# Second cross attention of a two-block network: who issues the stores of the relative scores, and who multiplies one half in eight by the mask

## The chip, the cores and the metric

The kernel runs on one NeuronCore of a Trainium2 chip. The metric is the time of one execution on the device in microseconds. Three runs took 1361.1, 1364.61 and 1364.95 us; the median is 1364.61.

## The reference, cut to what matters

The network is one program: cross attention, linear attention, an attention with a mixture of experts, a second cross attention (relative positions, a mask), a multi-query attention and a second mixture. The change touches the fourth layer and, with one line, the second. What the fourth computes (x is 256 rows by 256, the context 4096 rows, 16 heads of 16 columns, float32):

```
q, k, v = x @ Wq + bq, y @ Wk + bk, y @ Wv + bv          # split into heads
content = einsum('bthd,bThd->bhtT', q + r_w_bias, k)
rel     = einsum('bthd,bThd->bhtT', q + r_r_bias, pe)    # pe from sinusoids @ Wp + bp
rel     = _relative_shift(rel)    # pad one column left, read the same memory with another row length
attn    = (content + rel) / sqrt(16)
attn    = attn * mask - 1e10 * (1 - mask)
out     = softmax(attn) @ v       # then @ Wo + bo
```

In the second layer (linear attention) the line moved is the addition of the norm's bias `beta` to x, which may be done at any time before the normed result is added.

## The kernel before, in words

The second cross attention is `cross1`. Its work is cut into 64 units: 16 heads, two blocks of 128 query rows, two halves of 2048 keys (`HALF`). `where(p, c)` gives for a unit its number n, its head and its place u = 0 to 3 in the head (U = 4). Each unit is handled in two parts of 1024 keys (`SUB`), part 0 and part 1.

All engines run the same list of slots (`slots`): slots -4 to 3 written out, then a hardware loop of six turns with eight slots each, then slots 52 to 67 written out. There is no planner: the order inside a slot is written by hand, per engine. In slot n:

- TensorE (`slot` at L1842): relative scores of unit n+3, part 1; content scores of unit n, part 0; for one unit in four the projection of new queries (L1800); the joining of the sums of unit n-4; transposes (`turn`, L1817) of unit n-3, part 0; relative scores of unit n+4, part 0; content scores of unit n, part 1; transposes of unit n-3, part 1; the product with the values (`weigh`, L1830) for both parts. The relative scores go to the PSUM tile `rel_ps`, the content scores to `cont_ps`, the transposes to `turn_ps`; there is one tile of each.
- ScalarE (L1911): copies the transposes of unit n-3, part 0 (L1909); the relative scores of unit n+4, part 0 (L1898); the transposes, part 1; the exponential of unit n-1 over both parts (L1903); the relative scores of unit n+4, part 1; for one unit in four turned weights (L1930).
- VectorE (L2013): sums of unit n-4 (L2005); adds content scores to the relative scores read back, unit n, part 0 (`add`, L1980); maximum of unit n-1, part 0, with the term of the mask added (`top_of`, L1991, a custom operation); keeps sums; add of unit n, part 1; maximum of unit n-1, part 1; joins both maxima and turns the sign (L1997), which releases the exponential; for one unit in four makes queries (L2052).
- GpSimd (L1943): multiplies both parts of unit n by the mask in SBUF (L1950), each when its add is done.
- SyncE: the relative shift is done through DRAM. `store` (L1713) writes a unit's relative scores with a row length of 4097, `read_back` (L1700) reads them with a row length of 4096 into `row`. In slot n SyncE reads back part 0 of unit n+2 (after the stores of its head that it overlaps have landed), then waits for ScalarE's copy and stores unit n+4, then reads back part 1 of unit n+2. Loads of keys and values stand between.

Before slot 0 VectorE copies the right halves of the relative scores itself (`evacuate_right`) and in slot -1 computes the second half of `minus`, the mask's additive term. At the end the last two units (`at_end`) have the transposes of part 1 in `rel_ps`, and VectorE copies them (L2042).

In `linear_attn` VectorE rotates the keys, adds a bias to the values, adds `beta` to x (L1061), waits for the query activation and rotates the queries.

## Time and profile before

| | |
|---|---|
| median of 3 runs | 1364.61 us (1361.1 to 1364.95) |
| profiled execution | 1368.14 us, span 1366.3 us |
| second cross attention, unit stage | about 707 to 1209 us of the span |
| busy in the span: TensorE, VectorE, ScalarE, GpSimd | 1127.7, 822.7, 893.6, 632.3 us |
| mean granted TensorE clock | 0.931 |

The table of an execution gives for each engine how long it was busy over the whole span of six layers with different limits. For a stage, the windows and the timeline are read instead: a row of a timeline has the start, the duration, the engine and the line, and, in brackets, how long the engine stood idle before and who released it. A duration on VectorE or GpSimd can contain time in which the operation was already issued and did not yet proceed.

### The profile page before, as it was taken

Reading aid. Unit: us, or ns where it says so; the run is one execution under the profiler, and the core shown is the slowest. Engines: PE = TensorE matmul, PEld = TensorE weight load, DVE = VectorE, ACT = ScalarE, POOL = GpSimd, SP = SyncE. Lnnn points to the kernel's source line nnn. Section 1 sums busy time; section 2 is a strip of 40 time slices with the busy share of each in tenths; the row PEclk is TensorE's granted clock in tenths of the full one; section 3 lists DMA queues with packets and bytes.
Section 4 is the critical chain, followed back from the end, with each engine's and each line's share of the span. In section 5 each row is a group of like instructions: output and inputs, shape, how many; then the busy total and the mean of one; then the engine's idle time right before and its main releaser. Section 6 shows DMA issues by size and latency. Waiting matters only on the chain. (4 is left out here: it accounts for less than half of the span.)

```text
span 1366.3 us, 25496 instructions
## 1 busy us (share of the span) xinstructions
PE 1127.7 (83%) x8423; PEld 690.0 (50%) x8423; DVE 822.7 (60%) x1502; ACT 893.6 (65%) x1204; POOL 632.3 (46%) x297
## 2 busy tenths in 40 slices
PE   7677877859999859989977888888888888857798
PEld 3344443433444346678852444544455444434687
DVE  5688888870111166462235787888878888835312
ACT  3599999978999624433323788888888888524110
POOL 2277887850000005000004899999999999800000
PEclk9899999979999878989985899999999999878899
DMA  7875555538654070024458999999899999433140
GB/s 244 246 231 130 132 122 130 131 98 165 119 99 89 13 254 8 1 78 153 154 218 283 309 308 323 325 333 325 311 319 334 328 322 317 152 114 127 47 139 8
DMA packets 97052, 257.53 MB, mean 188 GB/s; under 512 B 11193, under 2 KB 41306, under 8 KB 85467
## 3 DMA queue, kind: packets, MB, share of 16 engines
q1 hardware_dynamic: 96992, 256.79, 60.3%
q8 instruction: 32, 0.52, 0.2%
q14 instruction: 28, 0.22, 0.1%
HBM read 165.31 MB, written 91.92 MB: 188 GB/s over the span
## 5 line engine op out<-in xcount | busy, mean ns | idle before, releaser
L1950 POOL TENSOR_TENSOR xb_row<-xb_row,w_mask 128x1024 f32<-128x1024 f32 x128 | 419.2, 3287 | 240.0 <-DVE xb_row L1980 238.7
L1980 DVE TENSOR_TENSOR xb_row<-xb_cont_ps,xb_row 128x1024 f32<-128x1024 f32 x128 | 156.7, 1224 | 83.2 <-PE xb_cont_ps L1773 73.3
L1773 PE MATMUL xb_rel_ps<-xb_kk,xb_qq 32*128 32x512 f32 x496 | 148.9, 678 | 35.0 <-ACT xb_out L1898 33.3
L561 DVE TENSOR_REDUCE xa_stats<-xa_b_ps 128x1 f32<-128x1024 f32 x128 | 155.8, 1219 | 27.2 <-PE xa_b_ps L477 25.8
L1991 DVE CUSTOM_DVE_ANT_0 xb_row<-xb_row,xb_minus 128x1024 f32<-128x1024 f32 x128 | 170.9, 1335 | 0.0
L1903 ACT ACTIVATE xb_row<-xb_row,xb_ntop 128x2048 f32<-128x2048 f32 x64 | 128.3, 2005 | 51.1 <-DVE xb_ntop L1997 51.1
L1773 PE MATMUL xb_cont_ps<-xb_kk,xb_qq 32*128 32x512 f32 x528 | 160.2, 684 | 1.5 <-DVE xb_qq L2052 1.1
L880 ACT ACTIVATE xa_probs<-xa_psT,xa_t_now 128x1024 f32<-128x1024 f32 x128 | 141.2, 1114 | 18.4 <-PE xa_psT L837 18.3
L1898 ACT COPY xb_out<-xb_rel_ps 128x1024 f32<-128x1024 f32 x124 | 124.7, 1005 | 39.8 <-PE xb_rel_ps L1773 26.8
L1909 ACT COPY xb_turned<-xb_turn_ps 128x1024 f32<-128x1024 f32 x126 | 127.5, 1012 | 26.9 <-PE xb_turn_ps L1817 24.8
L529 ACT ACTIVATE xa_exps<-xa_b_ps,xa_stats 128x1024 f32<-128x1024 f32 x128 | 140.7, 1102 | 6.6 <-DVE xa_stats L561 6.6
L1817 PEld LDWEIGHTS xb_turn_ps<-_ident,xb_row 128*128 128x128 f32 x1008 | 116.4, 149 | 56.0 <-issue 56.0
L1817 PE MATMUL xb_turn_ps<-_ident,xb_row 128*128 128x128 f32 x1008 | 139.3, 283 | 5.5 <-ACT xb_turned L1909 4.6
L647 POOL TENSOR_TENSOR xa_rest<-xa_exps 128x1024 f32<-128x1024 f32 x48 | 90.9, 1894 | 92.0 <-ACT xa_exps L529 86.7
L1830 PE MATMUL xb_sum_ps<-xb_turned,xb_vhead 128*17 128x128 f32 x2048 | 82.2, 279 | 37.1 <-ACT xb_turned L1909 36.0
L1420 POOL TENSOR_TENSOR b_tc<-b_raw,w_waves 128x512 f32<-128x512 f32 x4 | 5.1, 1274 | 216.1 <-ACT b_raw L1406 216.1
L477 PE MATMUL xa_b_ps<-xa_k,xa_q 96*128 96x512 bf16 x256 | 70.6, 388 | 24.3 <-ACT xa_exps L529 13.9
L539 ACT ACTIVATE xa_squares<-xa_exps 128x1024 f32<-128x1024 f32 x80 | 84.4, 1055 | 3.0
L810 PE MATMUL xa_sums<-xa_probs,xa_vhead 128*17 128x256 f32 x1024 | 81.1, 390 | 0.2 <-ACT xa_probs L880 0.2
L498 PE MATMUL xa_b_ps<-xa_wv,xa_ctxT 128*128 x512 | 67.3, 286 | 15.1 <-ACT xa_exps L529 15.1
L1830 PEld LDWEIGHTS xb_sum_ps<-xb_turned,xb_vhead 128*17 128x17 f32 x2048 | 45.5, 97 | 67.0 <-ACT xb_turned L1909 54.4
L498 PEld LDWEIGHTS xa_b_ps<-xa_wv,xa_ctxT 128*128 128x128 f32 x512 | 61.3, 196 | 31.0 <-ACT xa_exps L529 26.4
(367 smaller groups left out, 1823.9 us busy)
## 6 DMA issues: line engine op xcount, KB each, us to landing
xb_row<-rel_scores SPq DMA_DIRECT2D x128, 512.0 KB, 6.3
rel_scores<-xb_out SPq DMA_DIRECT2D x32, 1024.5 KB, 5.6
rel_scores<-xb_out SPq DMA_DIRECT2D x32, 1024.0 KB, 5.6
b_e_w<-in_L_ffn_e_w SPq DMA_DIRECT2D x32, 513.0 KB, 3.4
w_w<-in_L_ffn_w SPq DMA_DIRECT2D x24, 512.0 KB, 4.9
xa_k<-first_parts SPq DMA_DIRECT2D x24, 384.0 KB, 5.1
value_rows<-xa_values SPq DMA_DIRECT2D x16, 544.0 KB, 6.1
xb_kk<-key_blocks SPq DMA_DIRECT2D x17, 512.0 KB, 7.8
```

Of the source, the lines that this page charges most:

```text
L498: mm = nc.tensor.matmul(out[:, n * P:(n + 1) * P], ctxT[:, k, at:at + P], wv[:, bass.ds(it, 1), k, :], start=(k == 0), stop=(k == KC - 1))
L529: nc.scalar.activation(exps[:, u % 4], ps[:, slot % 4], ACT.Exp, scale=-1.0, bias=stats[:, c % 2, 0, u:u + 1], accum_out=stats[:, c % 2, 1 ...
L561: nc.vector.tensor_reduce(stats[:, c % 2, 0, u:u + 1], ps[:, slot % 4], AX, ALU.min).then_inc(s["min_ready"], 1)
L880: nc.scalar.activation(probs[:, g % 4].rearrange("p c n -> p (c n)"), ps[:, g % 2], ACT.Exp, scale=t_now[:, b:b + 1]).then_inc(probs_ready, 1)
L1773: mm = nc.tensor.matmul(out[:, k * BANK:(k + 1) * BANK], qq[rows, b, kind, t * P:(t + 1) * P], kk[rows, b, half], start=True, stop=True)
L1817: mm = nc.tensor.transpose(out_ps[:, k * P:(k + 1) * P], row[:, held(c), at:at + P], f.ident[:])
L1830: mm = nc.tensor.matmul(sum_ps[at:at + DV, 0:P], vhead[:, b, half * NCH // 2 + part * CPS + k, :], turned[:, part, k, :], start=(part == 0 ...
L1903: nc.scalar.activation(row[:, held(c)], row[:, held(c)], ACT.Exp, bias=ntop[:, u:u + 1]).then_inc(s["exp_done"], 1)
L1909: nc.scalar.copy(turned[:, part].rearrange("p k n -> p (k n)"), turn_ps[:]).then_inc(turned_sb[part], 1)
L1950: nc.gpsimd.tensor_tensor(row[:, held(c), at:at + SUB], row[:, held(c), at:at + SUB], mask[:, t, half * HALF + at:half * HALF + at + SUB], ...
L1980: nc.vector.tensor_tensor(row[:, held(c), at:at + SUB], cont_ps[:], row[:, held(c), at:at + SUB], ALU.add).then_inc(s["cont_out"], 1)
L1991: nc.vector.tensor_tensor_reduce(out=row[:, held(c), at:at + SUB], in0=row[:, held(c), at:at + SUB], in1=minus[:, t, half * HALF + at:half ...
```

## The change

- SyncE no longer stores the relative scores. ScalarE issues the store of unit n+4 in slot n, after its second copy of that unit's relative scores, and first waits for that copy (and, for the first four units, for VectorE's). SyncE's slot holds both read-backs one behind the other, and the loads as before.
- For the last unit of each head (u = 3), part 1, VectorE adds the content scores in PSUM (`cont_ps`), waits for itself, and multiplies the sum by the mask into `row`; GpSimd leaves that part out. That is one of eight halves of a head.
- The last slots: from slot 64 on, TensorE transposes both parts of a unit first in the slot. The last three units instead of two have part 1 in `rel_ps`; of these ScalarE copies the first, VectorE the last two.
- The second half of `minus` is computed in slot -4 instead of slot -1.
- In the linear attention the addition of `beta` stands ahead of the wait for the key activation.

```
--- before.py
+++ after.py
@@ -1052,13 +1052,13 @@
             step(nc.vector.tensor_scalar(red[:], red[:], PI_BELOW, -PI_BELOW, ALU.min, ALU.max))
...
             dve.wait_ge(s["loaded"], 80)
+            step(nc.vector.tensor_tensor(f.x[:], f.x[:], gain[:, 1].unsqueeze(1).to_broadcast([P, NT, D]), ALU.add))
             dve.wait_ge(s["k_gelu"], 1)
...
             dve.sem_inc(s["v_sb"], 1)
-            step(nc.vector.tensor_tensor(f.x[:], f.x[:], gain[:, 1].unsqueeze(1).to_broadcast([P, NT, D]), ALU.add))
             dve.wait_ge(s["q_gelu"], 1)
...
             dve.sem_inc(s["qrot_ready"], 1)
@@ -1625,7 +1625,7 @@
             names = ("small_loaded", "var_ready", "root_ready", "dve_steps", "xn_ready", "xnT_mm", "xnT_sb",
...
                      "rel_mm", "rel_out", "cont_mm", "cont_out", "masked", "halves_max", "top_ready",
-                     "exp_done", "turned", "weighed", "sums_sb", "gathered", "sums_read", "zero_set", "top_begun", "top_kept", "row_free")
+                     "exp_done", "turned", "weighed", "sums_sb", "gathered", "sums_read", "zero_set", "top_begun", "top_kept", "row_free", "added_here")
             s = {n: f.sem("b_" + n) for n in names}
...
             turned_sb = [f.sem(f"b_turned_sb{n}") for n in range(2)]
@@ -1683,7 +1683,15 @@
 
...
 
+                return isinstance(n, int) and n >= UNITS - 3
+
+            def by_vector(n):
+
                 return isinstance(n, int) and n >= UNITS - 2
+
+            def masked_here(u, part):
+
+                return u == U - 1 and part == 1
 
...
 
@@ -1710,19 +1718,6 @@
                     sp.dma_start(row[:, held(c):held(c) + 1, columns], src.rearrange("h p n -> p h n")
...
 
-                def store(p, c):
-                    n, head, u, b, t, half = where(p, c)
-                    sp.wait_ge(s["rel_out"], 2 * n + 3)
-                    if isinstance(n, int) and n < U:
-                        sp.wait_ge(s["fill_out"], n + 1)
-                    rows = rel_rows[bass.ds(head, 1), t * P:(t + 1) * P, :]
-                    if half == 0:
-                        dst, src = rows[:, :, 0:HALF + 1], out0
-                    else:
-                        dst, src = rows[:, :, HALF + 1:PITCH], out1
-                    sp.dma_start(dst.rearrange("h p n -> p (h n)"), src[:]).then_inc(rel_stored[u], 16)
-
-                rel_rows = rel_dram[:, 0:S * PITCH].rearrange("h (r n) -> h r n", n=PITCH)
                 shifted = rel_dram[:, S:S + S * S2].rearrange("h (r n) -> h r n", n=S2)
...
 
@@ -1738,15 +1733,9 @@
                         if n is None or n > U:
...
                         load_values(p, c + U)
-                    begins = n is not None and n == -2
                     if runs(n, 2):
-                        read_back(p, c + 2, 0, first=n is not None and n + 2 < ROWS_HELD)
-                    if runs(n, 2) and begins:
-                        read_back(p, c + 2, 1, first=True)
-                    if runs(n, U):
-                        store(p, c + U)
-                    if runs(n, 2) and not begins:
-                        read_back(p, c + 2, 1, first=n is not None and n + 2 < ROWS_HELD)
+                        for part in range(2):
+                            read_back(p, c + 2, part, first=n is not None and n + 2 < ROWS_HELD)
 
...
                     b = c // U % 2
@@ -1840,6 +1829,7 @@
                                      ).then_inc(s["gathered"], 1)
...
                 def slot(p, c, n):
+                    ending = isinstance(n, int) and n >= UNITS
                     if runs(n, U - 1) and (n is None or n > 0):
...
                     if c % U == 0 and (n is None or n < UNITS):
@@ -1849,6 +1839,9 @@
                         pe.wait_ge(k_loaded[(c // U + 1) % 2], 16 * (p + (c // U + 1) // 2 + 1))
...
                         content(p, c, 0)
+                    if ending and runs(n, -BEHIND):
+                        turn(p, c - BEHIND, 0)
+                        turn(p, c - BEHIND, 1)
                     if runs(n, -BEHIND - 1):
...
                     if n is None or n >= 0:
@@ -1856,7 +1849,7 @@
                             make_queries(2 * p + c // U + 2, c // U % 2)
...
                         bring_together(p, c - BEHIND - 1)
-                    if runs(n, -BEHIND):
+                    if runs(n, -BEHIND) and not ending:
                         turn(p, c - BEHIND, 0)
...
                         relative(p, c + U, 0)
@@ -1867,7 +1860,8 @@
                     if runs(n, 0):
...
                     if runs(n, -BEHIND):
-                        turn(p, c - BEHIND, 1)
+                        if not ending:
+                            turn(p, c - BEHIND, 1)
                         weigh(p, c - BEHIND, 0)
...
 
@@ -1897,6 +1891,20 @@
                     first = isinstance(n, int) and n < U
...
 
+                rel_rows = rel_dram[:, 0:S * PITCH].rearrange("h (r n) -> h r n", n=PITCH)
+
+                def store(p, c):
+                    n, head, u, b, t, half = where(p, c)
+                    act.wait_ge(s["rel_out"], 2 * n + 3)
+                    if isinstance(n, int) and n < U:
+                        act.wait_ge(s["fill_out"], n + 1)
+                    rows = rel_rows[bass.ds(head, 1), t * P:(t + 1) * P, :]
+                    if half == 0:
+                        dst, src = rows[:, :, 0:HALF + 1], out0
+                    else:
+                        dst, src = rows[:, :, HALF + 1:PITCH], out1
+                    nc.scalar.dma_start(dst.rearrange("h p n -> p (h n)"), src[:]).then_inc(rel_stored[u], 16)
+
                 def exponentials(p, c):
...
                     act.wait_ge(s["top_ready"], n + 1)
@@ -1906,19 +1914,22 @@
                     n, head, u, b, t, half = where(p, c)
...
                     act.wait_ge(s["weighed"], 2 * n + part + 1)
-                    nc.scalar.copy(turned[:, part].rearrange("p k n -> p (k n)"), turn_ps[:]).then_inc(turned_sb[part], 1)
+                    src = rel_ps if at_end(n) and part == 1 else turn_ps
+                    nc.scalar.copy(turned[:, part].rearrange("p k n -> p (k n)"), src[:]).then_inc(turned_sb[part], 1)
 
...
                         evacuate(p, c + U, 0)
-                    if runs(n, -BEHIND) and not at_end(where(p, c - BEHIND)[0]):
+                    if runs(n, -BEHIND) and not by_vector(where(p, c - BEHIND)[0]):
                         copy_turned(p, c - BEHIND, 1)
...
                         evacuate(p, c + U, 1)
+                    if runs(n, U):
+                        store(p, c + U)
                     if turns_weights(n, c):
...
 
@@ -1945,11 +1956,14 @@
                         return
...
                     for part in range(2):
+                        if masked_here(u, part):
+                            continue
                         at = part * SUB
+                        halves_done = 2 if masked_here(u, part + 1) else 1
                         pool.wait_ge(s["cont_out"], 2 * n + part + 2)
...
                                                 mask[:, t, half * HALF + at:half * HALF + at + SUB],
-                                                ALU.mult).then_inc(s["masked"], 1)
+                                                ALU.mult).then_inc(s["masked"], halves_done)
 
...
 
@@ -1977,6 +1991,14 @@
                     dve.wait_ge(rel_back[u][part], 16 * (head + 1))
...
                     at = part * SUB
+                    if masked_here(u, part):
+                        nc.vector.tensor_tensor(cont_ps[:], cont_ps[:], row[:, held(c), at:at + SUB], ALU.add
+                                                ).then_inc(s["added_here"], 1)
+                        dve.wait_ge(s["added_here"], head + 1)
+                        nc.vector.tensor_tensor(row[:, held(c), at:at + SUB], cont_ps[:],
+                                                mask[:, t, half * HALF + at:half * HALF + at + SUB],
+                                                ALU.mult).then_inc(s["cont_out"], 1)
+                        return
                     nc.vector.tensor_tensor(row[:, held(c), at:at + SUB], cont_ps[:], row[:, held(c), at:at + SUB],
...
 
@@ -1984,6 +2006,8 @@
 
...
                     dve.wait_ge(s["masked"], 2 * n + part + 1)
+                    if masked_here(u, part):
+                        dve.wait_ge(s["cont_out"], 2 * n + part + 2)
                     if part == 0 and isinstance(n, int) and n == 0:
...
                     dve.sem_inc(s["top_begun"], 1)
@@ -2013,10 +2037,10 @@
                 def slot(p, c, n):
...
                         evacuate_right(c + U)
+                        if n == -U:
+                            set_minus(1)
                         if makes_queries(n, c):
                             make_queries(1, 1)
-                        if n == -1:
-                            set_minus(1)
                     if runs(n, -BEHIND - 1):
...
                     if runs(n, 0):
@@ -2032,7 +2056,7 @@
                     if n is None or n >= 0:
...
                             make_queries(2 * p + c // U + 2, c // U % 2)
-                    if runs(n, -BEHIND) and at_end(where(p, c - BEHIND)[0]):
+                    if runs(n, -BEHIND) and by_vector(where(p, c - BEHIND)[0]):
                         copy_last_turned(p, c - BEHIND)
```

## Rows read from the trace of the kernel before

**Rows 1.** Windows, one turn of the loop: stretch, length, busy us by engine, clock, DMA share, GB/s
```profile
922.40:979.30 56.90, 47.94 (x536) 28.14 (x536) 47.10 (x85) 47.57 (x43) 52.66 (x17) 1.00 0.94 325
```

**Rows 2.** Timeline, one slot: start us, us, engine line op out<-in, idle before it
```profile
930.00 0.19 PEld L1773 LDWEIGHTS xb_rel_ps<-xb_kk,xb_qq 32*128 32x128 f32 x2 [1.27 <-ACT xb_out L1898]
...
931.24 1.23 DVE L1980 TENSOR_TENSOR xb_row<-xb_cont_ps,xb_row 128x1024 f32<-128x1024 f32 x1 [0.97 <-PE xb_cont_ps L1773]
...
932.38 1.22 DVE L1991 CUSTOM_DVE_ANT_0 xb_row<-xb_row,xb_minus 128x1024 f32<-128x1024 f32 x1
...
933.64 0.21 DVE L1997 TENSOR_SCALAR xb_ntop<-xb_top 128x1 f32<-128x1 f32 x1
...
933.89 2.01 ACT L1903 ACTIVATE xb_row<-xb_row,xb_ntop 128x2048 f32<-128x2048 f32 x1 [0.67 <-DVE xb_ntop L1997]
...
935.80 0.99 ACT L1898 COPY xb_out<-xb_rel_ps 128x1024 f32<-128x1024 f32 x1
...
936.84 0.19 PEld L1773 LDWEIGHTS xb_rel_ps<-xb_kk,xb_qq 32*128 32x128 f32 x2 [0.48 <-ACT xb_out L1898]
```

**Rows 3.** The same timeline, from the next slot to the fourth exponential
```profile
937.00 1.01 ACT L1909 COPY xb_turned<-xb_turn_ps 128x1024 f32<-128x1024 f32 x1
...
938.15 1.06 PE L1817 MATMUL xb_turn_ps<-_ident,xb_row 128*128 128x128 f32 x8
...
939.25 1.81 DVE L1991 CUSTOM_DVE_ANT_0 xb_row<-xb_row,xb_minus 128x1024 f32<-128x1024 f32 x1
939.33 1.01 ACT L1909 COPY xb_turned<-xb_turn_ps 128x1024 f32<-128x1024 f32 x1 [0.21 <-PE xb_turn_ps L1817]
...
940.97 0.70 PE L1773 MATMUL xb_cont_ps<-xb_kk,xb_qq 32*128 32x512 f32 x2
...
941.35 2.00 ACT L1903 ACTIVATE xb_row<-xb_row,xb_ntop 128x2048 f32<-128x2048 f32 x1 [1.01 <-DVE xb_ntop L1997]
...
942.02 0.73 PEld L1800 LDWEIGHTS xb_both<-xb_xnT,xb_wturn 128*128 128x128 f32 x4 [0.76 <-issue]
...
943.13 1.07 PE L1817 MATMUL xb_turn_ps<-_ident,xb_row 128*128 128x128 f32 x8
...
944.31 0.70 PE L1773 MATMUL xb_rel_ps<-xb_kk,xb_qq 32*128 32x512 f32 x2
...
948.22 2.00 ACT L1903 ACTIVATE xb_row<-xb_row,xb_ntop 128x2048 f32<-128x2048 f32 x1 [0.55 <-DVE xb_ntop L1997]
...
955.49 2.01 ACT L1903 ACTIVATE xb_row<-xb_row,xb_ntop 128x2048 f32<-128x2048 f32 x1 [0.94 <-DVE xb_ntop L1997]
```

**Rows 4.** Timeline of GpSimd where the stage starts
```profile
737.89 2.34 POOL L1950 TENSOR_TENSOR xb_row<-xb_row,w_mask 128x1024 f32<-128x1024 f32 x1 [1.12 <-DVE xb_row L1980]
741.36 3.25 POOL L1950 TENSOR_TENSOR xb_row<-xb_row,w_mask 128x1024 f32<-128x1024 f32 x1 [1.13 <-DVE xb_row L1980]
```

**Rows 5.** Page, part 5: GpSimd's mask products, out<-in xcount, busy, mean ns
```profile
L1950 POOL TENSOR_TENSOR xb_row<-xb_row,w_mask 128x1024 f32<-128x1024 f32 x128 | 419.2, 3287 | 240.0 <-DVE xb_row L1980 238.7
```

**Rows 6.** Timeline of SyncE's queue: a store, a load of keys
```profile
951.29 0.35 SPq L1723 DMA_DIRECT2D rel_scores<-xb_out  x1
...
966.71 1.15 SPq L97 DMA_DIRECT2D xb_kk<-key_blocks  x1
```

**Rows 7.** Timeline of the last slots
```profile
1167.10 1.23 DVE L1980 TENSOR_TENSOR xb_row<-xb_cont_ps,xb_row 128x1024 f32<-128x1024 f32 x1 [1.74 <-DMA xb_row<-rel_scores]
...
1189.15 2.15 DVE L1991 CUSTOM_DVE_ANT_0 xb_row<-xb_row,xb_minus 128x1024 f32<-128x1024 f32 x1
...
1197.49 2.00 ACT L1903 ACTIVATE xb_row<-xb_row,xb_ntop 128x2048 f32<-128x2048 f32 x1
...
1208.43 0.17 DVE L2010 TENSOR_SCALAR xb_o_all<-xb_both 128x17 f32<-128x17 f32 x1 [0.49 <-PE xb_both L1839]
```

**Rows 8.** Timeline of linear attention
```profile
484.94 0.43 DVE L1024 SCALAR_TENSOR_TENSOR la_kr<-la_k,la_rope 128x256 f32<-128x256 f32 x1 [1.54 <-ACT la_k L1012]
...
488.66 0.69 DVE L1061 TENSOR_TENSOR _x<-_x,la_gain 128x512 f32<-128x512 f32 x1
```

More of the change, by code:

```diff
@@ L1054, in _ @@
             dve.wait_ge(s["loaded"], 80)
+            step(nc.vector.tensor_tensor(f.x[:], f.x[:], gain[:, 1].unsqueeze(1).to_broadcast([P, NT, D]), ALU.add))
             dve.wait_ge(s["k_gelu"], 1)
@@ L1060, in _ @@
             dve.sem_inc(s["v_sb"], 1)
-            step(nc.vector.tensor_tensor(f.x[:], f.x[:], gain[:, 1].unsqueeze(1).to_broadcast([P, NT, D]), ALU.add))
             dve.wait_ge(s["q_gelu"], 1)
@@ L1740, in slot @@
                         load_values(p, c + U)
[L1741 removed]
                     if runs(n, 2):
[L1743 to L1749 removed]
+                        for part in range(2):
+                            read_back(p, c + 2, part, first=n is not None and n + 2 < ROWS_HELD)
                 def load_values(p, c):
@@ L1851, in slot @@
                         content(p, c, 0)
+                    if ending and runs(n, -BEHIND):
+                        turn(p, c - BEHIND, 0)
+                        turn(p, c - BEHIND, 1)
                     if runs(n, -BEHIND - 1):
@@ L1858, in slot @@
                         bring_together(p, c - BEHIND - 1)
-                    if runs(n, -BEHIND):
+                    if runs(n, -BEHIND) and not ending:
                         turn(p, c - BEHIND, 0)
@@ L1908, in copy_turned @@
                     act.wait_ge(s["weighed"], 2 * n + part + 1)
-                    nc.scalar.copy(turned[:, part].rearrange("p k n -> p (k n)"), turn_ps[:]).then_inc(turned_sb[part], 1)
+                    src = rel_ps if at_end(n) and part == 1 else turn_ps
+                    nc.scalar.copy(turned[:, part].rearrange("p k n -> p (k n)"), src[:]).then_inc(turned_sb[part], 1)
                 def slot(p, c, n):
@@ L1915, in slot @@
                         evacuate(p, c + U, 0)
-                    if runs(n, -BEHIND) and not at_end(where(p, c - BEHIND)[0]):
+                    if runs(n, -BEHIND) and not by_vector(where(p, c - BEHIND)[0]):
                         copy_turned(p, c - BEHIND, 1)
@@ L1921, in slot @@
                         evacuate(p, c + U, 1)
+                    if runs(n, U):
+                        store(p, c + U)
                     if turns_weights(n, c):
```

63 lines of the change are left out of this document (37 added, 26 removed).

## The prediction, made before the changed kernel was run

> **What bounds the kernel now.** I read the page's totals first. No engine is busy for the whole span, so the share of busy time decides nothing, and the stretch that the change touches has to be read by itself: the second cross attention, 707 to 1209 us, and in it the even part from 765 to 1165 us. The table by windows shows one turn of its loop of eight units (the other five from 808 to 1150 us are alike): 56.9 us, 28.45 us for one round of four units (one head), TensorE's clock at its upper level (granted 1.00), VectorE 47 us busy, ScalarE 47.5, TensorE 48, GpSimd 52.7, DMA 94% [rows 1]. At first sight GpSimd and the DMA engines are the wall. The timelines of single engines show something else.
>
> *The loop of waits.* I followed one slot back from what ended its waits [rows 2]. TensorE's relative and content scores of one half start at 930.00; VectorE adds the content scores at 931.24, takes the maximum at 932.38, joins the halves at 933.64; ScalarE's exponential starts at 933.89, its copy of the relative scores at 935.80, and TensorE's next pair of scores, which needs the PSUM tile that this copy empties, at 936.84, "waiting for ACT xb_out". Each step starts when the one before ends. It is a closed loop, once per slot, and one turn is 936.84 - 930.00 = 6.84 us. Nothing in it is GpSimd's or a DMA. Four turns are 27.36 of the 28.45 us of a round.
>
> *What is on top of it.* The other start of the exponential in these rows is 7.46 later (933.89 to 941.35), then 6.87 (948.22) and 7.27 (955.49) [rows 3]. In the long slots the maximum takes 1.81 instead of 1.22 [rows 2, 3]. Its partner is GpSimd's product with the mask: 2.34 us while VectorE takes no maxima, 3.25 once it does [rows 4]. So the maximum (two SBUF inputs) and the mask product take turns: one slot costs the pair 2 x 1.22 + 2 x 2.34 = 7.12 us, which is 56.9/8 = 7.11. The add of a PSUM and an SBUF operand beside the same GpSimd work stays at 1.22 [rows 2, 3]. The Trainium skill says so too ("SBUF — State Buffer", section "Who interferes with whom" and the one on the two sides of SBUF): VectorE and GpSimd share one pair of ports as an exclusive lock, a VectorE operation with two SBUF inputs takes it, the loser is blocked whole. By that rule alone the change is worth its lock time; it makes the rival A below, and the trace agrees with the lock (0.91 us more on each mask product) but not with the conclusion: the loop of 6.84 is there with the lock free.
>
> *A second chain.* Between the slots of units 0 and 1 of a head TensorE is tight as well [rows 3]: scores at 936.84, ScalarE's copy of turned weights 937.00 (ends 938.01), transposes 938.15, copy 939.33, scores 940.97, query projection 942.02, transposes 943.13 to 944.20, next pair of scores 944.31. That is 7.47 us with no gap over 0.25.
>
> **The change part by part.**
>
> *The product on VectorE (16 units, the second half of the last unit of each head).* Removed: 16 of GpSimd's 128 mask products, 3.29 us each by their mean [rows 5]. GpSimd is on the path only through the lock. Added, between the add and the maximum of the unit before, on the very loop of 6.84: one more VectorE operation from PSUM and SBUF to SBUF, and a wait for the add. The like of it is the add, 1.22 us; adjacent VectorE operations start 1.14 apart (931.24 to 932.38 [rows 2]), and a wait for one's own predecessor gives up that overlap and some hundredths: I take 1.30, bounds 1.14 and 1.40. Behind it on VectorE stand the maximum and the joined maximum, and ScalarE's exponential waits for them. ScalarE idles 0.67 us before that exponential, but it idles *for* this chain, so that idle time hides nothing. VectorE's own idle time of 0.97 us lies before the add, while it waits for TensorE, and can't be used either. So the slot of the fourth unit goes from 6.84 to 8.14.
>
> *What the lock gives back.* In the slot of unit 3 the maximum waited for nothing (1.22), so there is nothing to give. The slot after it (unit 0) loses its wait for the lock, 1.81 - 1.22 = 0.59, because GpSimd has no second product to do and the add comes early. But the second chain holds that slot at 7.47, so the gain is 0. In the slot of unit 2 the add is late because two query operations stand ahead of it; its maximum keeps its wait (the slot is 7.27, 955.49 - 948.22). Bounds: 0 to 0.43 a round, if that wait goes too; I take 0.
>
> *ScalarE issues the stores.* SyncE's issue of this very store takes 0.35 us [rows 6]. On ScalarE it stands after the second copy of relative scores, waits for that copy to be finished, and then the copy of turned weights follows. The trace shows no DMA issued by ScalarE; I take 0.35 and 0.10 for the wait, 0.45. Bounds: 0.05 (only the wait, an issue that the engine's data path doesn't see) and 1.25 (SyncE's issue of keys is 1.15 [rows 6], and 0.10). It isn't on the loop of 6.84: the pair of scores starts meanwhile. In most slots it eats ScalarE's idle time. In the slot of unit 0 it is on the second chain, ahead of the copy at 937.00, less some 0.05 of gap before the transposes: 7.47 + 0.40 = 7.87. SyncE loses 64 issues and its waits for the copies; the read-backs go out sooner. VectorE waits for a read-back hardly ever (the adds wait for TensorE), and the DMA engines carry the same bytes, so the even part gains nothing by it. The Trainium skill ("DMA: Bandwidth & Descriptors", on issuing engines not being separate queues) says that issuing from a second engine saves only the sequencer's time. No row here has a second queue, and the sum doesn't use it.
>
> *Sum of a round:* unit 0 7.87, unit 1 6.87, unit 2 7.27 (both as they are), unit 3 8.14, together 30.15 against 7.47 + 6.87 + 7.27 + 6.84 = 28.45. That is +1.70. The even part, 765 to 1165, is 400/28.45 = 14 rounds: +23.8 us. The bounds: product 1.14, store nothing, lock wait of unit 2 gone: +0.71, 14 times is +10. Product 1.40, store 1.25: the second chain takes 1.15 and the slots of units 1 and 2 lose their slack of about 0.3 each: 1.40 + 1.15 + 0.6 = +3.1, 14 times is +44; I hold that the copy's issue is near the store's own row and keep about +35 as the upper end.
>
> *Start.* The slot of the first head's unit 3 gets its product outside of the 14 rounds: +1.3. The second computation of "minus" moves from slot -1 to slot -4. It is one operation of about the length of VectorE's wait there for TensorE, and the first add followed TensorE's scores, not it: 0.
>
> *Last slots.* The exponential of unit 62 starts at 1191.59 behind a maximum that took 2.15 [rows 7]: the product ahead of it adds 1.3 and takes most of that wait, so it starts at about 1192.3. Then on ScalarE its 2.0 and two copies of 1.0 (the second no longer waits for the first, since unit 61 now uses both PSUM tiles): the last exponential starts at 1196.3 instead of 1197.49. Weighing of unit 61 ends at 1197.0, two transposes of 1.07 at 1199.2, VectorE's copy and the weighing at 1201.2, transposes of unit 63 at 1203.4, copy 1.22, weighing, sums and joining another 2.1: the last operation ends at 1206.7 instead of 1208.6 [rows 7]. That is -1.9, bounds 0 and -3. The add at 1167.10 waits 1.74 us for a read-back [rows 7]; SyncE issues it sooner now, as it no longer waits for copies: -1.7, bounds 0 and -1.8.
>
> *Linear attention.* The bias added to x (0.69 us) moves from between two steps of the path, into a wait of 1.54 us for the key activation [rows 8]: -0.7, bounds 0 and -0.7.
>
> Total: +23.8 + 1.3 - 1.9 - 1.7 - 0.7 = +20.8 us. The profiled execution took 1368.1 us (span 1366.3 and 1.8 around it) and would take 1389. It is 3.5 us above the median of the runs shown, 1364.6. I take the difference over to the median: 1385.4 us, +1.5%.
>
> **The rivals.**
>
> A. *The lock and GpSimd were the wall.* If each slot's length is the lock's time, a round loses 2 mask products of 2.34 out of eight units, so 2.34 in a round: 26.1; the DMA engines at 94% set a floor of 0.94 x 28.45 = 26.7. Gain 1.7 a round, 24 in all, and 3 at the ends: 1338 us. If it goes only as far as the loop of 6.84 (27.36 a round, the product hidden), the gain is 15 + 3: 1346. For it: 7.12 against 7.11, GpSimd 92% busy. Against it: a slot with an undisturbed maximum has no idle step in the loop, and the product is laid on it. It is right from the point where VectorE can do the product before its content scores would be late anyway.
>
> B. *Nothing measurable.* With the low bounds (+10) and the ends giving more than I count (-6 with their bounds, +1.3 for the first head less), or the second chain closing up because its copy finds ScalarE free earlier: about +2, 1367 us.
>
> C. *The store on ScalarE is dear.* An issue of about 1.2 us instead of 0.35, since the two queues' issues get in each other's way or the address work lands on ScalarE: +35, less 3 at the ends: 1397 us. For it: SyncE's issues reach 1.15 [rows 6]. Against it: the store's own issues there are all near 0.35.
>
> D. *The product does not reach the loop because the transfers set the pace after all* (94% share): then every slot stays at 7.11 and only the ends change: 1361 us. Against it: the waits of the adds are for TensorE.
>
> **How the numbers follow.** Forecast case 0.64, A 0.09, B 0.10, C 0.13, D 0.04. What a measurement of this kernel can tell from no change is 0.3%, 4 us. Faster: A and a quarter of D, 0.10. Same: B, most of D, 0.11 with a rest from the low side. Slower: 0.79. Range: it leaves out A (0.09), D (0.04) and the far half of C (0.07): from 1365, just under B, to 1397 in C.
>
> **What would show it.** Right: exponentials 8.1 us apart in each fourth slot, with an operation of about 1.22 us from xb_cont_ps between add and maximum, and maxima of 1.22 in that slot; a loop of eight units of about 60.3 us; GpSimd's products 112 instead of 128 and its busy share down with no time won; more idle time of VectorE's adds for TensorE in the slot of unit 1; a gap of 0.4 to 0.5 ahead of the first copy of turned weights. Wrong: fourth slots at 7.1 or below (then the product is hidden and A holds), a loop below 56 us, or ScalarE gaps of over 1 us at the stores (C).

## The result, and the profile after

The changed kernel took 1405.49 us (median of 4 runs, 1400.25 to 1416.43), the kernel before 1364.34 us (4 runs): ratio 1.0309, 95% interval 1.0281 to 1.0337. That is 41 us more, where 20.8 were forecast; the time lies above the range of 1365 to 1397. The direction was right; the forecast size was half of the measured one. The profiled execution after has a span of 1405.5 us (1366.3 before), 39.2 us more.

Page after: busy time of each engine (part 1), two DMA queues with their packets, MB and share of 16 engines (part 3), GpSimd's mask products (part 5):

```profile
PE 1140.9 (81%) x8423; PEld 695.0 (49%) x8423; DVE 845.2 (60%) x1518; ACT 892.6 (64%) x1204; POOL 578.4 (41%) x281
...
q1 hardware_dynamic: 87776, 189.66, 45.4%
q10 hardware_dynamic: 9216, 67.13, 11.8%
...
L1964 POOL TENSOR_TENSOR xb_row<-xb_row,w_mask 128x1024 f32<-128x1024 f32 x112 | 365.3, 3275 | 335.1 <-DVE xb_row L2002 335.0
```

GpSimd has 112 products instead of 128 [rows 5] and 54 us less to do, and nothing came of it. VectorE has 22 us more. The stores have a queue of their own, q10.

**Where the 39.2 us are.** The slot of unit n is here the time from the exponential of unit n-2 to that of unit n-1; four slots are a round (one head). I took the start of every exponential in both traces. Unit 3's is at 770.32 before and 769.08 after; unit 59's, 14 rounds later, at 1169.74 and 1209.80. So the 14 rounds took 399.4 us before and 440.7 after: +41.3. The last slots (unit 59 to unit 63) took 27.75 and 29.68: +1.9. What lies ahead of unit 3's exponential and behind unit 63's gives 1.2 and 2.8 back. The loss is all in the loop, about 2.95 a round where I had 1.70.

One round after, timeline, rows chosen (start, duration, engine, line, operation, in brackets the idle time before and who ended it). To be compared with [rows 2, 3]:

```profile
902.00 2.00 ACT L1911 ACTIVATE xb_row<-xb_row,xb_ntop 128x2048 f32<-128x2048 f32 x1 [0.48 <-DVE xb_ntop L2021]
...
903.91 0.99 ACT L1892 COPY xb_out<-xb_rel_ps 128x1024 f32<-128x1024 f32 x1
904.26 1.22 DVE L2002 TENSOR_TENSOR xb_row<-xb_cont_ps,xb_row 128x1024 f32<-128x1024 f32 x1 [0.94 <-DMA xb_row<-rel_scores]
...
905.07 0.34 ACTq L1906 DMA_DIRECT2D rel_scores<-xb_out  x1
...
905.54 1.13 PE L1762 MATMUL xb_cont_ps<-xb_kk,xb_qq 32*128 32x512 f32 x4
...
905.61 1.01 ACT L1918 COPY xb_turned<-xb_turn_ps 128x1024 f32<-128x1024 f32 x1 [0.70 <-ACT xb_out L1892]
...
906.71 1.22 DVE L2002 TENSOR_TENSOR xb_row<-xb_cont_ps,xb_row 128x1024 f32<-128x1024 f32 x1
...
907.85 2.07 DVE L2015 CUSTOM_DVE_ANT_0 xb_row<-xb_row,xb_minus 128x1024 f32<-128x1024 f32 x1
...
910.21 2.01 ACT L1911 ACTIVATE xb_row<-xb_row,xb_ntop 128x2048 f32<-128x2048 f32 x1 [1.26 <-DVE xb_ntop L2021]
...
914.40 1.23 DVE L1995 TENSOR_TENSOR xb_cont_ps<-xb_cont_ps,xb_row 128x1024 f32<-128x1024 f32 x1 [1.08 <-PE xb_cont_ps L1762]
...
915.67 1.23 DVE L1998 TENSOR_TENSOR xb_row<-xb_cont_ps,w_mask 128x1024 f32<-128x1024 f32 x1
...
916.81 1.22 DVE L2015 CUSTOM_DVE_ANT_0 xb_row<-xb_row,xb_minus 128x1024 f32<-128x1024 f32 x1
...
918.32 2.01 ACT L1911 ACTIVATE xb_row<-xb_row,xb_ntop 128x2048 f32<-128x2048 f32 x1 [1.16 <-DVE xb_ntop L2021]
...
925.41 2.01 ACT L1911 ACTIVATE xb_row<-xb_row,xb_ntop 128x2048 f32<-128x2048 f32 x1
...
933.32 2.01 ACT L1911 ACTIVATE xb_row<-xb_row,xb_ntop 128x2048 f32<-128x2048 f32 x1 [0.49 <-DVE xb_ntop L2021]
```

Three things are to be seen.

- *The product.* Add at 914.40, product at 915.67, maximum at 916.81: 1.27 and 1.14. The slot of unit 3, from exponential to exponential, is 918.32 - 910.21 = 8.11 us; the forecast was 8.14.
- *ScalarE's issue.* The copy of relative scores ends at 904.90, the issue stands at 905.07 and takes 0.34, and the copy of the transposes starts only at 905.61, "waiting for ACT xb_out" 0.70. I had taken 0.45. The slots of units 0 and 1 together are 933.32 - 918.32 = 15.00 instead of the 14.74 forecast.
- *The read-backs.* In the slot of unit 2 the add waits 0.94 us for a read-back (904.26). The content scores of the other part need the PSUM tile that this add empties (905.54), the second add follows them at 906.71, and the whole slot is 910.21 - 902.00 = 8.21 instead of the 7.27 forecast. Before, the like add waits for nothing:

```profile
921.09 1.23 DVE L1980 TENSOR_TENSOR xb_row<-xb_cont_ps,xb_row 128x1024 f32<-128x1024 f32 x1
```

  7.27 + 0.94 is 8.21. This wait was in no term of my sum. Between 765 and 1160 us eleven adds wait for a read-back after the change, 11.5 us in all, and all eleven stand in the slot of unit 2, one in nearly every round.

**SyncE and the queues.** Waits from 765 to 1160 us (in total, times, the longest), after:

```profile
SPq L1715 <- DMA rel_scores<-xb_out: 291.9, 37, 9.9
...
DVE xb_row L2002 <- DMA xb_row<-rel_scores: 11.5, 11, 2.0
```

The same of before:

```profile
SPq L1707 <- DMA rel_scores<-xb_out: 142.4, 41, 5.2
SPq L1723 <- ACT xb_out L1898: 97.6, 50, 5.3
...
DVE xb_row L1980 <- DMA xb_row<-rel_scores: 7.5, 8, 1.3
```

SyncE did lose its waits for ScalarE's copies (97.6 us), as forecast. But its waits for stores to *land* before it can read them back grow by more than that (292 instead of 142, the longest 9.9 instead of 5.2). The DMA issues of the same stretch (KB each, median us from issue to landing), after:

```profile
xb_row<-rel_scores SPq DMA_DIRECT2D x100, 512.0 KB, 5.8
rel_scores<-xb_out ACTq DMA_DIRECT2D x26, 1024.0 KB, 6.6
rel_scores<-xb_out ACTq DMA_DIRECT2D x25, 1024.5 KB, 6.0
```

and before:

```profile
xb_row<-rel_scores SPq DMA_DIRECT2D x111, 512.0 KB, 6.3
rel_scores<-xb_out SPq DMA_DIRECT2D x28, 1024.5 KB, 5.6
rel_scores<-xb_out SPq DMA_DIRECT2D x28, 1024.0 KB, 5.6
```

The read-backs land a little sooner, the stores later. One store after: issued at 921.38, landed about 930.1, 8.7 us later; SyncE had issued a load of keys at 921.03. The queues in the first four us of its flight, and in the next three:

```profile
q1 hardware_dynamic: 284, 1.00, 82.8%
...
q10 hardware_dynamic: 100, 0.82, 62.3%
q1 hardware_dynamic: 226, 0.44, 38.2%
```

From 921.4 to 925.4 only SyncE's queue moved data, and none of the store's; from 925.4 to 928.5 the engines served both queues. So the store's own data started about 4 us behind its issue. The read-back that needs this store went out at 930.30. Sharing by itself isn't new: before, 1.71 MB went through the one queue while a store of 1 MB was in flight (908.6 to 914.2), and that store landed after 5.6 us.

### The profile page after: what moved, and what is told of

It reads as the page before. It is cut to its first block and busy times, and to the rows that moved or that the text cites. A ratio compares the mean times of both kernels' runs of the same rounds, so it can differ in the third digit from the quotient of the medians.

```text
span 1405.5 us, 25513 instructions
## 1 busy us (share of the span) xinstructions
PE 1140.9 (81%) x8423; PEld 695.0 (49%) x8423; DVE 845.2 (60%) x1518; ACT 892.6 (64%) x1204; POOL 578.4 (41%) x281
## 5 line engine op out<-in xcount | busy, mean ns | idle before, releaser
L1964 POOL TENSOR_TENSOR xb_row<-xb_row,w_mask 128x1024 f32<-128x1024 f32 x112 | 365.3, 3275 | 335.1 <-DVE xb_row L2002 335.0
L2002 DVE TENSOR_TENSOR xb_row<-xb_cont_ps,xb_row 128x1024 f32<-128x1024 f32 x112 | 137.2, 1225 | 75.8 <-PE xb_cont_ps L1762 59.0
L1892 ACT COPY xb_out<-xb_rel_ps 128x1024 f32<-128x1024 f32 x124 | 125.0, 1008 | 27.9 <-PE xb_rel_ps L1762 21.8
L1819 PE MATMUL xb_sum_ps<-xb_turned,xb_vhead 128*17 128x128 f32 x2048 | 86.9, 291 | 36.9 <-ACT xb_turned L1918 34.9
L1762 PEld LDWEIGHTS xb_rel_ps<-xb_kk,xb_qq 32*128 32x128 f32 x496 | 39.8, 194 | 76.7 <-ACT xb_out L1892 58.0
```

The source lines that it names most:

```text
L1762: mm = nc.tensor.matmul(out[:, k * BANK:(k + 1) * BANK], qq[rows, b, kind, t * P:(t + 1) * P], kk[rows, b, half], start=True, stop=True)
L1819: mm = nc.tensor.matmul(sum_ps[at:at + DV, 0:P], vhead[:, b, half * NCH // 2 + part * CPS + k, :], turned[:, part, k, :], start=(part == 0 ...
L1892: nc.scalar.copy(out[:, part * SUB:(part + 1) * SUB], rel_ps[:]).then_inc(s["rel_out"], 2 if first else 1)
L1964: nc.gpsimd.tensor_tensor(row[:, held(c), at:at + SUB], row[:, held(c), at:at + SUB], mask[:, t, half * HALF + at:half * HALF + at + SUB], ...
L2002: nc.vector.tensor_tensor(row[:, held(c), at:at + SUB], cont_ps[:], row[:, held(c), at:at + SUB], ALU.add).then_inc(s["cont_out"], 1)
```

## The experiments

All ratios are against the kernel before, run beside it on the same chip, with a 95% interval; a difference between two experiments of different groups (e1 to e4; e5, e6, e7, e9; e8, e10, e11, e12; the changed kernel) is between kernels timed apart. "14 rounds" is the time from unit 3's exponential to unit 59's in the profiled execution, 399.4 us before.

**e1_product: the product on VectorE alone.** As the change's parts in `masked_here`, `add`, `top_of` and GpSimd's loop; SyncE stores.

> Only the product with the mask of one half in eight moves to VectorE; everything else as before. Theory 1 (the product lies on the closed loop scores, add, maximum, exponential, copy): the slot of the fourth unit 8.1 us, the loop of eight units 59 to 60 us instead of 56.9, in all about +19 us: 1384. Rival A (lock and GpSimd set the pace): the loop gets shorter, 1340 to 1350.

1386.83 us, ratio 1.0174 (1.0141 to 1.0206), 14 rounds 420.4. The product costs 23 us.

**e2_store: the stores on ScalarE alone**, with SyncE's two read-backs one behind the other.

```
-                    if runs(n, U):
-                        store(p, c + U)             # SyncE
+                        store(p, c + U)             # ScalarE, after evacuate(p, c + U, 1)
```

> Only the issuer of the stores and the order of the read-backs on SyncE change. Theory 1 with the size read from the changed kernel (0.8 us of ScalarE instead of 0.45): the second chain 0.75 longer in one slot of four, about +11: 1375. Rival S (the transfers themselves come late, because the store on its own queue shares the DMA engines with the read-backs and the keys): +20 or more, 1384 or above, and adds that wait for read-backs. If neither matters: 1364.

1397.48 us, ratio 1.0239 (1.0212 to 1.0267), 14 rounds 428.1. The part that I had priced at 5.6 us costs 33.6 by itself. The adds wait 20.2 us for read-backs (7.5 before). That is what rival S said, not theory 1.

**e3_rest: last slots, `minus`, `beta` alone.**

> Only the last slots, the time at which minus is computed, and the place of the addition of beta. Predicted -1.9, 0 and -0.7, so about 1361.5; if the rest of these edits costs something in the sum of the whole change: 1366 or more.

1360.82 us, ratio 0.9976 (0.9962 to 0.9990), 14 rounds 399.4. It gains 3 us, about what those terms gave together (-1.9, -0.7).

**e4_small: the issue without the transfer.** SyncE keeps the stores; ScalarE issues an 8 KB transfer at the place of the store.

```
+                    act.wait_ge(s["rel_out"], 2 * n + 3)
+                    nc.scalar.dma_start(scratch[...], wq[0:16, 0, 0:P]).then_inc(s["small_out"], 16)
```

> The kernel before, and ScalarE also issues, where the changed kernel has its store, a transfer of 8 KB to a scratch tensor, with the same wait for its own copy. SyncE keeps the real stores. So ScalarE's cost of an issue is there and the large transfers stay in one queue. If the cost is ScalarE's time: as e2. If it is the order of the transfers: +11 at most, 1375, and e2 above it.

1384.51 us, ratio 1.0150 (1.0128 to 1.0172), 14 rounds 416.8: 20.6 us for issues that move next to nothing. That is neither of the expected results: more than +11, less than e2. No add waits for a read-back. Timeline of ScalarE:

```profile
927.84 0.99 ACT L1898 COPY xb_out<-xb_rel_ps 128x1024 f32<-128x1024 f32 x1
928.99 0.32 ACTq L1903 DMA_DIRECT2D scratch<-xb_wq  x1
929.51 1.01 ACT L1915 COPY xb_turned<-xb_turn_ps 128x1024 f32<-128x1024 f32 x1 [0.68 <-ACT xb_out L1898]
930.41 1.03 ACT L1898 COPY xb_out<-xb_rel_ps 128x1024 f32<-128x1024 f32 x1
```

From the end of the copy (928.83) 0.16 to the issue, 0.32 of issue, 0.20 to the next copy. The last two copies, with nothing between, start 0.90 apart though one lasts 1.01. So the issue costs 0.68 + 0.1, about 0.78 us of ScalarE. By the wait in this row, it delays the copy of the transposes, behind that the next copy of relative scores, and with it TensorE's next scores, and not in the slots of units 0 and 1 alone: these take 9.8 us more in the 14 rounds, and the slot of unit 3, which has no slack, 7.5 more (from 6.84 to about 7.4 each). The slot of unit 2 stays as it is (102.6 and 102.5).

**e5_order: the order of SyncE alone.** SyncE issues both read-backs, then the store, all in one queue.

> The kernel before; on SyncE both read-backs stand ahead of the store in every slot, instead of one on each side of it. ScalarE is untouched and all transfers stay in one queue. If the 13 us that the real stores cost more than the small ones (e2 against e4) come from the order in which SyncE reads back: slower by 8 or more, and adds that wait for read-backs. If they come from the second queue: within 4 us of before.

1432.75 us, ratio 1.0498 (1.0480 to 1.0515). Stores land after 7.8 and 8.0 us (medians) instead of 5.6, ScalarE's copies into the buffer that a store reads wait 51.3 us for landings, and adds wait 25.3 us for read-backs. This order also sends each store later, behind SyncE's waits, and TensorE's granted clock is lower (0.909 over the span, 0.93 before), so it isn't the order of e2 by itself. It shows only that late landings can be worth more than any issue here.

**e6_store_wait: e2 with the old order in time.** SyncE waits for ScalarE's copy ahead of its second read-back, as it did when it stored.

```
+                    if runs(n, U):
+                        sp.wait_ge(s["rel_out"], 2 * where(p, c + U)[0] + 3)
```

> As e2, but SyncE reads back the second part only after the copy that ScalarE's store waits for, so that the read-backs keep the times that they had. ScalarE's cost and the second queue stay. If the order and time of the read-backs make the 13 us: as e4, 1384. If two queues that share the DMA engines make them: as e2, 1397.

1393.06 us, ratio 1.0214 (1.0174 to 1.0254). That lies between the two expected results, nearer to e2: 27.9 us above its own before where e2 was 33.6 above its own. The intervals of the two overlap and the 14 rounds are no shorter (429.5 against 428.1), so no effect of the order is shown. Against e4, 7 to 9 us stay with the order of before; they come with the real store on its own queue.

**e7_small_late: e4's issue ahead of the exponential**, one slot later, where ScalarE idles.

```
                         copy_turned(p, c - BEHIND, 1)
+                    if runs(n, U - 1):
+                        small_store(p, c + U - 1)
                     if runs(n, -1):
                         exponentials(p, c - 1)
```

> As e4, but the small transfer of ScalarE stands one slot later, behind the second copy of the transposes and ahead of the exponential, where ScalarE stood idle for 0.5 to 1.1 us. Theory (what costs is the 0.8 us ahead of the first copy, which the transposes wait for): most of e4's +20 is gone, 1364 to 1369. Rival (an issue on ScalarE costs the same wherever it stands): 1384.

1365.92 us, ratio 1.0003 (0.9986 to 1.0019), 14 rounds 403.0. The same 64 issues cost nothing that can be measured in the median. Timeline of ScalarE, one slot:

```profile
926.37 1.01 ACT L1915 COPY xb_turned<-xb_turn_ps 128x1024 f32<-128x1024 f32 x1
926.59 0.32 ACTq L1903 DMA_DIRECT2D scratch<-xb_wq  x1
928.36 2.01 ACT L1909 ACTIVATE xb_row<-xb_row,xb_ntop 128x2048 f32<-128x2048 f32 x1 [0.97 <-DVE xb_ntop L2006]
```

Here nothing holds the issue back: it passes while the copy is still running (926.59 in 926.37 to 927.38), and the exponential waits for VectorE anyway. In e4 it waits for the copy of relative scores that stands right ahead of it, as the true store must.

**e9_deferred: the product off the loop.** VectorE multiplies that part in SBUF after it has joined the maxima of the unit before, behind what releases the exponential.

```
                         top_of(p, c - 1, 1)
+                    if runs(n, 0) and masked_here(c % U, 1):
+                        product(p, c)
```

> The product of e1 on VectorE, now from SBUF and behind the joined maximum that releases the exponential, so off the closed loop; GpSimd has the same 112 products as in e1. Theory (e1's +23 come from the product's place on the loop): 1360 to 1369. Rival (VectorE has no room for it, or the port that it then takes): 1380 or more. If the lock set the pace: 1350 or less.

1367.29 us, ratio 1.0014 (1.0005 to 1.0024). The same 16 products cost 2 us instead of 23. (The profiled execution was the slowest of the ten, 1371.31, with 14 rounds of 404.6.) GpSimd has as many fewer as after the change, and the time isn't below before. Timeline of VectorE in e9:

```profile
905.08 1.22 DVE L2008 CUSTOM_DVE_ANT_0 xb_row<-xb_row,xb_minus 128x1024 f32<-128x1024 f32 x1
...
906.34 0.21 DVE L2014 TENSOR_SCALAR xb_ntop<-xb_top 128x1 f32<-128x1 f32 x1
...
906.59 1.22 DVE L1994 TENSOR_TENSOR xb_row<-xb_row,w_mask 128x1024 f32<-128x1024 f32 x1
907.92 1.22 DVE L1987 TENSOR_TENSOR xb_row<-xb_cont_ps,xb_row 128x1024 f32<-128x1024 f32 x1
```

The joined maximum (906.34) is out before the product starts. Rival A is refuted: less work for GpSimd buys nothing. The product on VectorE takes 1.22 us instead of the 2.34 of GpSimd's; had the lock set the pace, even the difference would have been worth about 1.1 us a round, some 15 us (an estimate from these rows).

**e12_product_rest and e8_after_small: the change taken apart from the top.** e12 is the changed kernel with SyncE's stores and order of before. e8 is e12 with e4's small issue on ScalarE.

> The changed kernel without any of the store's edit: product, last slots, minus and beta. If the parts add up (e1 +23, e3 -3): 1384. The rest of the changed kernel's +41 is then the store's, about 21, less than the 33 that it costs alone, because the slot with the product hides a part of it.

> The changed kernel, but with the stores back on SyncE in the old order, and the small transfer of e4 where ScalarE's store stood. If the changed kernel's long slot of unit 2 (8.2 us) comes from late read-backs: 7.3 to 7.5 there and 1390 to 1393 in all. If it comes from ScalarE's issue together with the product: as the changed kernel, 1405.

e12: 1385.72 us, ratio 1.0146 (1.0111 to 1.0182), 14 rounds 420.4. e8: 1392.96 us, ratio 1.0216 (1.0195 to 1.0236), 14 rounds 430.5. Four exponentials in a row, timelines of ScalarE, e12:

```profile
911.84 2.01 ACT L1916 ACTIVATE xb_row<-xb_row,xb_ntop 128x2048 f32<-128x2048 f32 x1 [1.86 <-DVE xb_ntop L2024]
918.68 2.01 ACT L1916 ACTIVATE xb_row<-xb_row,xb_ntop 128x2048 f32<-128x2048 f32 x1 [0.39 <-DVE xb_ntop L2024]
926.10 2.01 ACT L1916 ACTIVATE xb_row<-xb_row,xb_ntop 128x2048 f32<-128x2048 f32 x1 [0.47 <-DVE xb_ntop L2024]
933.43 2.02 ACT L1916 ACTIVATE xb_row<-xb_row,xb_ntop 128x2048 f32<-128x2048 f32 x1 [1.09 <-DVE xb_ntop L2024]
```

and e8:

```profile
916.08 2.01 ACT L1922 ACTIVATE xb_row<-xb_row,xb_ntop 128x2048 f32<-128x2048 f32 x1 [1.12 <-DVE xb_ntop L2033]
923.21 2.01 ACT L1922 ACTIVATE xb_row<-xb_row,xb_ntop 128x2048 f32<-128x2048 f32 x1
931.12 2.01 ACT L1922 ACTIVATE xb_row<-xb_row,xb_ntop 128x2048 f32<-128x2048 f32 x1 [0.48 <-DVE xb_ntop L2033]
```

In e12 the slots of units 0 and 1 are 6.84 and 7.42, together 14.26 (14.33 before [rows 2, 3]): the lock gives back 0.07. In e8 they are 7.13 and 7.91, together 15.04: the issue costs 0.78 there. Both kernels came out as expected (1384; 1390 to 1393). e8 has no add that waits for a read-back; after has 11.5 us of them. The 14 slots of unit 2 take 102.2 us in e8 and 114.6 after, +12.4; the other 42 slots together are 2.1 shorter after. So what the real store costs beyond the small one lies in the slot of unit 2, where those adds wait.

**e10_store_late and e11_after_moved: both parts at their better places.** e10 is e2 with the store issued in the next slot behind the first copy of transposes. e11 is the changed kernel with that and with e9's product.

```
                         copy_turned(p, c - BEHIND, 0)
+                    if runs(n, U - 1) and (n is None or n > 0):
+                        store(p, c + U - 1)
```

> The store edit alone, as in e2, but ScalarE issues the store in the next slot, right behind its first copy of the transposes, so that this copy isn't delayed. If ScalarE's time ahead of that copy is the larger part of e2's +33: 1374 to 1380, with the share of the second queue left (9 to 13). If the place doesn't matter: 1397. If the later store delays the tile's next use: above 1397.

> The changed kernel with both parts at another place: the product behind the joined maximum (e9), the store behind the first copy (e10). Theory: the places are what costs, so most of the +41 is gone and what the second queue costs is left: 1371 to 1378. If the parts cost something wherever they stand: 1395 or more.

e10: 1390.34 us, ratio 1.0205 (1.0180 to 1.0229). e11: 1395.80 us, ratio 1.0223 (1.0191 to 1.0254). Both miss the low figures expected (1374 to 1380, 1371 to 1378); e11 is at its high one. Taking the issue off the loop didn't save the store: it goes out later and lands no sooner after its issue (medians of e10 7.4 and 5.1 us for the two sizes, of e2 7.4 and 5.4), and the adds wait 31.5 us in e10 and 31.1 in e11. In e11's profiled execution 34.5 us are the last slots, with the granted clock at 0.50 from 1205 to 1230 us. Waits of e11, 765 to 1160 us:

```profile
DVE xb_row L1996 <- DMA xb_row<-rel_scores: 31.1, 13, 3.5
```

The best of all kernels is e3, 3 us below before.

## Why the prediction was wrong, point by point

From the profiled executions, 14 rounds: 399.4 (before), 420.4 (e12, product and rest), 430.5 (e8, an issue on ScalarE beside it), 440.7 (after, the real store on its own queue). By medians: +21.8 (e12 against before, 1363.91 in its runs), +7.2, and +12.5 to the changed kernel (timed apart, against 1364.34). My sum had 16.9 for the first, 3.9 for the second (the issue's 5.6 less the 1.7 at 1167.10), and nothing for the third. The real store costs as much more than the small one without the product: 13.0 from e4 to e2.

- **The closed loop of 6.84 and the product on it: right.** 8.11 for 8.14, in after, e8 and e12 alike. e9 shows why: off the loop the same product is worth 2 us. An undisturbed round of e12 is 29.70 us, +1.25 over 28.45 (forecast +1.30).
- **The clock: a term at nothing, without a reason.** Before, in windows of 5 us the granted clock is 1.00 from 765 to 1170 us. In the 14 rounds of e12 it falls four times, to between 0.66 and 0.77. Two windows of e12 (us, busy time of TensorE, its weight loads, VectorE, ScalarE and GpSimd, then granted clock, DMA share, GB/s):

```profile
1030.00:1035.00 5.00, 3.25 (x26) 1.39 (x18) 3.26 (x9) 4.12 (x4) 2.85 (x1) 0.91 0.83 297
1035.00:1040.00 5.00, 4.55 (x53) 2.71 (x49) 2.99 (x6) 3.75 (x3) 3.68 (x2) 0.75 0.97 318
```

  The fall (a part of the window at 1.2 GHz, before and behind it 2.4) comes behind a slot with the product, in which TensorE was busy 3.25 of 5 us; in the rounds before the change it was busy 336 of 400. The next two slots took 7.54 and 7.91 instead of 6.84 and 7.42. The 14 rounds of e12 are 420.4 - 14 x 29.70 = 4.6 us above undisturbed ones. After has five such falls in its rounds (windows at 860, 1040, 1065, 1080 and 1135, down to 0.66 to 0.70), and a longer one from 1205 us on. The window of after:

```profile
1210.00:1220.00 10.00, 10.00 (x58) 5.50 (x58) 5.24 (x9) 3.53 (x3) 5.79 (x3) 0.50 0.81 306
```

  There unit 60's exponential comes 10.39 us behind unit 59's (6.97 before), which is why the last slots show +1.9 where -1.9 was forecast; e12, without it, has 25.0 against 27.75. That the clock doesn't fall before and does after is seen; that TensorE's longer idle time is the cause was not tried by itself. The length of a round alone doesn't decide it: the rounds of e2 and e4 are 2.05 and 1.24 us longer than before and show no fall, those of e9, whose median round is as before, show two.
- **The store's issue on ScalarE, 0.45: mis-sized, and partly misplaced.** It is 0.78. I counted the row of SyncE's issue and 0.10 for the wait; missing were 0.2 between the issue and the next operation, and the 0.1 by which adjacent copies otherwise overlap. And I let it count in the slot of unit 0 alone: 0.40 a round, 5.6 in all. Beside the product it counts 0.78 in a round (e8; 7.2 us by medians, 10 by the profiled rounds), by itself in the slot of unit 3 as well (e4, 20.6 us). In the changed kernel the product covers that second place (the slot of unit 3 is 8.11 with the issue and without it), and that is nearly all of what the parts (23 + 33.6 - 3 = 53.6) have above 41: e1, e4 and e3 add up to 40.6, and e8, which has all three, is 29.1 above its before.
- **"The read-backs go out sooner. ... so the even part gains nothing by it": the step that failed.** I looked at the bytes and at the issues, and took the landing of the stores for unchanged without a row on it. More than half of the difference that was missing (20 us) is here: 12.5 us from e8 to after. The read-backs of one store's rows can't go out before it has landed (the waits of SyncE at L1715). From its issue to the first of its 8 KB packets a store took 0.86 us in the median and at most 1.3 in e8, 1.94 and at most 4.4 after; to its landing 5.1 and 6.05, at most 7.3 and 9.4 (packets and landings of the traces, 765 to 1160 us). SyncE waits up to 9.9 us for a landing, and the adds in the slot of unit 2 wait 0.5 to 2.0, and in the round shown 0.94 of wait is 0.94 of slot. The sum of such waits isn't the loss everywhere: e7 and e9 have 14.4 and 15.5 us of them, and their rounds are only 3.5 and 5.2 longer. The Trainium skill ("DMA: Bandwidth & Descriptors", on issuing engines not being separate queues) says that transfers of several issuing engines interleave on the same DMA engines and save only sequencer time. The trace agrees with the interleaving (0.82 MB of one queue and 0.44 of the other from 925.4 to 928.5); I took from the rule only that nothing is won, not that something can be lost.
- **Rival C** named the store as dear and gave 1397, but by an issue of about 1.2 us, and the issue takes 0.34; its mechanism isn't there. **Rival A** is refuted by e9, **B** and **D** by the result. Of D this much is true: the transfers don't set the pace by their bytes (DMA share 0.93 before, 0.81 after), but some of them do by their landing once it is later.
- **The second chain: its length right, a row misread.** The copy at 937.00 that I called the copy of turned weights is the copy of transposes (`xb_turned`), and between the copy at 939.33 and the scores at 940.97 the chain also has the first product with the values, at 940.39, which the rows shown leave out. Without the store's issue the two slots that it spans stayed at 14.26 (e12), though it is the slot of unit 1 and not that of unit 0 that is the long one there (7.42 and 6.84).
- **Lock:** 0 forecast, 0.07 a round in e12 (that the lock gives it is argued, not shown). The maximum in the slot of unit 2 kept its wait (2.07 after), as forecast.
- **Ends:** e3 gains 3 us in the median, -2.6 were given for last slots and `beta`. The -1.7 for the add at 1167.10 can't be told: such waits became more, not fewer (1.53 us in one add at 1188.91 after).

What stays open: why a store lands later on its own queue. Two things are seen after the change: its data start later, behind what SyncE issued just before, and then both queues are served at once. e6 speaks for the second: with SyncE's old order the first packet comes 0.97 us behind the issue in the median, nearly as in e8, and the store still lands only after 6.7 us. Whether it would land as early as before if the second queue held it alone, with the read-backs held back, wasn't tried.

## What to carry to other kernels

In a chain of transfers in which one may only go out when another has landed, the order in the queue is part of the schedule: before moving one of them to another engine's queue, look at who waits for its landing and how long that wait already is, not only at bytes and issue time. An issue on a compute engine cost its row and the gap around it (here 0.34 became 0.78), and nothing that could be measured at a place where the engine idled and the wait ahead of it was already met (e7); so find the place first. Work laid on the closed loop of this kernel cost its full length, the same work beside it nearly nothing: e1 against e9.

## What the runs showed of the hardware

- A DMA issued by ScalarE takes 0.32 to 0.39 us in its queue; behind a wait for its own copy, the copy of transposes starts 0.68 to 0.71 after that copy's end (after, e4), where adjacent copies otherwise overlap by 0.1.
- A 1 MB store in SyncE's queue, in the old order, landed after 5.6 us in the median before and after 4.8 to 5.4 in e12 and e8, after 6.0 to 6.6 (after) and 5.4 to 7.4 (e2) on ScalarE's, after 7.8 to 8.0 us in one queue behind two read-backs (e5).
- A store on ScalarE's queue can stand for 4 us without a packet while the other queue's transfers run (after, 921.4 to 925.4: 1.00 MB on q1, none on q10).
- A wait for one's own predecessor on VectorE, where the first operation writes PSUM and the second reads it, cost 0.13 us, start to start: add to product 1.27, product to maximum 1.14.
- TensorE's granted clock stayed at its upper level through the whole loop before, in e2 and in e4, and fell in it for a few us at a time in e1 and e12 (four times each), after (five), e9 (two) and e7 (one). In after, GpSimd's and the DMA engines' load had gone down meanwhile (GpSimd busy 289 instead of 365 of 395 us, DMA share 0.81 instead of 0.93).
